# A graph layer and its feed-forward on one core: the neighbour sums of a block in two halves, in three bursts a slot, and a sixth of the rescalings on VectorE

## The chip, the cores and the metric

One core of a Trainium2 chip runs the kernel. The metric is device time in microseconds of one launch, over several runs. The profile is one profiled execution of the same program; its times are counted from its first instruction.

## What is computed

6250 nodes have 512 features each. 106,250 edges (50,000 random ones in both directions, and one from each node to itself) are sorted by their destination, so a node has 17 on average. Two layers follow each other:

```
xn  = layernorm(x)
agg = segment_sum(xn[src], dst);  neigh = agg / max(deg, 1)
h   = layernorm(xn @ W_self + b_self + neigh @ W_neigh) * gamma + beta
h   = where(h >= 0, h, 0.25 * h) + xn
x1  = x + h
y   = layernorm(x1)
out = x1 + (silu(y @ q(w_gate).T) * (y @ q(w_up).T)) @ q(w_down).T
```

`q` rounds each group of 128 weights to -1, 0 or 1 times the group's mean size. The feed-forward is 512 to 1408 to 512. Inputs and output are float32.

## The kernel before

**Blocks and slots.** The nodes are cut into 49 blocks of 128. A first stage (to about 205 us) normalises each block, multiplies it by `W_neigh` on TensorE in float32 (line 807) and writes the result to a table in HBM, split into a high and a low float16 part (2 x 512 values a node). The same stage turns the quantised weights around and finds, for each block, the first edge that ends in it (`edge_ranges`, VectorE, whose passes over 125 x 2450 values stand between blocks 9 and 16). Then come 49 slots `t`, one for each block, of 18 ticks `k`, and some more without a block. A slot is an order of work, not a time: each engine walks the same ticks and waits on semaphores.

**The sums of a block.** 2304 edges (18 tiles of 128, `STEPS`) cover a block. SyncE loads their sources (`idx`) and destinations (`dstv`) two slots ahead. GpSimd gathers one row of the table for each edge, by one indirect DMA for each tile (line 759), into `rows`, which holds 18 tiles: tile `j` of the next block may start when TensorE has used tile `j` of this one (`p_used`, in pairs). VectorE makes the one-hot matrix `hot` of the destinations (line 1293; 128 x 2304), and adds it up into `degs` in three reductions (line 1303). TensorE multiplies, for each tile, the one-hot matrix (as weights, 128 columns) with the high and with the low half of the gathered rows and adds both up in the bank `agg_ps` (lines 889 and 891): 36 products of 512 columns a block. `AGG_AT` spreads the 18 tiles over the ticks 2 to 17. At the next slot's tick 0 VectorE takes the sum out of the bank (line 1475, `v_h0`), which the first product of the next block waits for; then come the two norms of the block, and DMA transposes that put it into `x1T`.

**The feed-forward.** It runs on chunks of four blocks (512 columns; the first chunk has one block), interleaved with the sums. Each 128-row group of weights has its own scale, so a sum is built in a PSUM bank of `LANES` = 6 in turn: a step is two products (high and low part, lines 994 and 995) onto the bank, then the bank is multiplied by the ratio of two scales (line 1088 on ScalarE; line 1432 on VectorE, which does 2 of 5 only after the last block's slot), then the bank's next step may come. A list `FSTEPS` holds the steps, and `PACE` and `EVEN` (38 and 35 a slot) say to which tick each is assigned; a chunk can't begin before its last block is in `x1T`, and the list leaves a gap in the slot where nothing is ready. Products with `W_self` (line 807, float32) and the transposes of finished results (line 934) run among these steps. In slots 0 to 4 the place of the feed-forward is taken by 23 blocks of `W_self` products (`HELD_IN`).

## Time and profile before

| | us |
|---|---|
| median of 3 runs (lowest, highest) | 1694.86 (1693.52, 1698.13) |
| span of the profiled execution | 1674.1 |
| first stage | to about 205 |
| the block sums taken from the bank, first and last | 245.2 and 1552.6 |
| TensorE, VectorE, ScalarE, GpSimd busy | 1537.9, 1055.9, 1177.1, 938.3 |

The profiled span is 20.8 us under the median; that much lies around it. A product's duration (0.38 us) is its way through the array; products start closer together than that, so what TensorE can do is read from starts. A float32 product has two records. A GpSimd record is the writing of one gather's descriptors, and not the gather.

### The profile page before, as it was taken

How to read it: one execution, taken by the hardware profiler on the slowest of the kernel's cores; microseconds unless marked ns; L12 is line 12 of the kernel's file. 1: busy time of each engine (PE TensorE's matmuls, PEld its weight loads, DVE VectorE, ACT ScalarE, POOL GpSimd, SP SyncE). 2: the span in 40 equal slices, each digit the busy share in tenths (PEclk: the TensorE clock that was granted, in tenths of full speed). 3: DMA queues.
4: the chain of work that ended last, by engine and by line, in shares of the span. 5: the costliest groups of instructions: out<-in, count | busy, mean ns of one | idle time of the engine just before them, and what ended most of it. 6: DMA issues, size and time to landing. Idle time of an engine off the chain costs nothing.

```text
span 1674.1 us, 21796 instructions
## 1 busy us (share of the span) xinstructions
PE 1537.9 (92%) x6421; PEld 750.7 (45%) x6422; DVE 1055.9 (63%) x2305; ACT 1177.1 (70%) x2248; POOL 938.3 (56%) x936
## 2 busy tenths in 40 slices
PE   7999989987889999999999998999998998989897
PEld 3444434444444454444444444444444443444343
DVE  8999624655565565564665756557466466573876
ACT  5577500026777787778787786869887887879796
POOL 2123277666676666666666766667666666764000
PEclk9999989989998999999999999999999999999999
DMA  9869488997776887777777867787777777784101
GB/s 303 257 219 292 125 293 313 274 282 208 213 226 189 225 224 221 218 229 210 216 212 226 228 201 230 209 235 211 217 209 223 218 213 223 206 228 129 38 14 37
DMA packets 210883, 353.40 MB, mean 211 GB/s; under 512 B 105482, under 2 KB 105482, under 8 KB 210754
## 3 DMA queue, kind: packets, MB, share of 16 engines
q0 software_dynamic: 70560, 231.27, 47.4%
q1 hardware_dynamic: 140204, 120.73, 24.5%
q8 instruction: 52, 0.85, 0.2%
q14 instruction: 67, 0.55, 0.1%
HBM read 295.79 MB, written 39.62 MB: 200 GB/s over the span
## 4 chain that ended last, share of the span: by engine, by line
PE 84%; issue 6%; ACT 6%; DVE 2%; DMA 1%; another core or an unknown queue 0%; DVEq 0%; SPq 0%; ACTq 0%
PE f_ps L994 21%; PE f_ps L995 20%; PE f_ps L807 20%; PE agg_ps L889 10%; PE agg_ps L891 10%; ACT f_ps L1088 4%; PE side_ps L934 1%; PE agg_ps L803 1%; PE side_ps L803 1%; PE f_ps L889 0%; PE f_ps L891 0%; ACT hT L1113 0%; ACT acc L1098 0%; DVE acc L1440 0%; DMA rows<-in_x 0%
## 5 line engine op out<-in xcount | busy, mean ns | idle before, releaser
L759 POOL DMA_INDIRECT rows<-node_table,idx x882 | 891.6, 1011 | 442.6 <-issue 241.3
L1088 ACT ACTIVATE f_ps<-f_ps,ratio 128x512 f32<-128x512 f32 (+2 forms) x1303 | 777.0, 666 | 240.6 <-PE f_ps L995 163.2
L994 PE MATMUL f_ps<-x1T,tern 128*128 128x512 f16 (+2 forms) x1144 | 424.2, 374 | 52.0 <-issue 28.2
L995 PE MATMUL f_ps<-x1T,tern 128*128 128x512 f16 (+2 forms) x1144 | 422.4, 372 | 0.0
L889 PE MATMUL agg_ps<-rows,hot 128*128 128x512 f16 x846 | 328.5, 388 | 22.8 <-issue 22.8
L891 PE MATMUL agg_ps<-rows,hot 128*128 128x512 f16 x846 | 326.1, 385 | 4.3 <-issue 4.3
L1440 DVE SCALAR_TENSOR_TENSOR acc<-f_ps,scl,acc 128x512 f32<-128x512 f32 (+2 forms) x143 | 102.4, 717 | 229.0 <-PE f_ps L995 116.4
L994 PE MATMUL f_ps<-hT,tern 128*128 128x512 f16 (+2 forms) x572 | 213.4, 376 | 25.6 <-issue 13.0
L995 PE MATMUL f_ps<-hT,tern 128*128 128x512 f16 (+2 forms) x572 | 212.6, 374 | 0.0
L994 PEld LDWEIGHTS f_ps<-x1T,tern 128*128 128x128 f16 x1144 | 113.1, 99 | 216.6 <-issue 67.2
L889 PEld LDWEIGHTS agg_ps<-rows,hot 128*128 128x128 f16 x846 | 120.1, 142 | 133.3 <-issue 64.2
L995 PEld LDWEIGHTS f_ps<-x1T,tern 128*128 128x128 f16 x1144 | 113.9, 100 | 109.6 <-issue 7.1
L891 PEld LDWEIGHTS agg_ps<-rows,hot 128*128 128x128 f16 x846 | 121.6, 144 | 84.0 <-issue 39.9
L1453 DVE TENSOR_TENSOR hT<-acc,hT 128x512 f16<-128x512 f32 (+2 forms) x143 | 93.5, 654 | 84.9 <-issue 47.1
L1303 DVE TENSOR_REDUCE degs<-hot 128x44 f16<-128x792 f16 x147 | 133.1, 944 | 0.0
L1098 ACT ACTIVATE acc<-f_ps,scl 128x512 f32<-128x512 f32 (+2 forms) x143 | 98.4, 693 | 28.7 <-PE f_ps L995 23.1
L807 PE MATMUL f_ps<-wself,xj 128*128 128x512 f32 x208 | 107.3, 597 | 2.9 <-issue 1.7
L994 PEld LDWEIGHTS f_ps<-hT,tern 128*128 128x128 f16 x572 | 56.7, 99 | 116.1 <-ACT f_ps L1088 39.9
L737 POOL TENSOR_TENSOR hsx<-hsx 128x512 f16<-128x512 f16 x33 | 38.7, 1175 | 102.5 <-DVE hsx L1266 58.9
L1129 ACT ACTIVATE work<-x,nmn,rsn 128x512 f32<-128x512 f32 x49 | 41.6, 849 | 74.4 <-issue 54.0
L1113 ACT ACTIVATE hT<-acc 128x512 f16<-128x512 f32 (+2 forms) x143 | 90.3, 631 | 2.7 <-DVE acc L1440 2.4
L995 PEld LDWEIGHTS f_ps<-hT,tern 128*128 128x128 f16 x572 | 57.2, 100 | 55.4 <-issue 4.9
(176 smaller groups left out, 1705.1 us busy)
## 6 DMA issues: line engine op xcount, KB each, us to landing
rows<-node_table,idx POOLq DMA_INDIRECT x882
hsx<-own_rows SPq DMA_DIRECT2D x49, 256.0 KB
hsx<-in_x SPq DMA_DIRECT2D x48, 256.0 KB
out_nodes<-work SPq DMA_DIRECT2D x48, 256.0 KB, 2.2
xj<-xnt_rows SPq DMA_DIRECT2D x26, 256.0 KB
node_table<-work SPq DMA_DIRECT2D x25, 256.0 KB, 3.1
acc<-own_rows SPq DMA_DIRECT2D x23, 256.0 KB
own_rows<-acc SPq DMA_DIRECT2D x23, 256.0 KB
```

Source lines behind the costliest of these rows:

```text
L759: pool.indirect_dma_start(out=rows[:, j, :], out_offset=None, in_=table[:, :], in_offset=bass.IndirectOffsetOnAxis(ap=of[:, j:j + 1], axis ...
L807: return pe.matmul(to[:, :], turned_rows[:, k, :], weight[:, k, :], start=(k == 0), stop=(k == KT - 1), skip_group_check=True)
L889: pe.matmul(agg[:, :], hot[:, b % 2, :, j], rows[:, j, 0:D], start=(j == 0), stop=False, skip_group_check=True)
L891: mm = pe.matmul(agg[:, :], hot[:, b % 2, :, j], rows[:, j, D:2 * D], start=False, stop=(j == STEPS - 1), skip_group_check=True)
L994: pe.matmul(to, lhs, parts[0], start=g == 0, stop=False, skip_group_check=True)
L995: pe.matmul(to, lhs, parts[1], start=False, stop=True, skip_group_check=True).then_inc(p_ff, 1)
L1088: act.activation(ps, ps, ACT.Copy, scale=ratio[:, w if up else 2, j:j + 1]).then_inc(a_scaled, 1)
L1098: act.activation(acc[:, 0, u % 2, 0:width], ps, ACT.Silu, scale=scl[:, 0, j:j + 1]).then_inc(a_silu, 1)
L1113: act.activation(hT[:, 0, f, 0:width], acc[:, 1, u % 2, 0:width], ACT.Copy).then_inc(a_hi, 1)
L1303: dve.tensor_reduce(degs[:, lo:hi], hot[:, b % 2, lo:hi, :], AX.X, ALU.add).then_inc(v_degs, 1)
L1440: dve.scalar_tensor_tensor(out=acc[:, 1, u % 2, 0:width], in0=ps, scalar=scl[:, 1, j:j + 1], in1=acc[:, 0, u % 2, 0:width], op0=ALU.mult, ...
L1453: dve.tensor_tensor(hT[:, 1, f, 0:width], acc[:, 1, u % 2, 0:width], hT[:, 0, f, 0:width], ALU.subtract).then_inc(v_hlo, 1)
```

## The change

A block's 128 nodes become two halves of 64 (`HALVES`). A half gets a window of 11 tiles: half 1 the tiles 7 to 17, half 0 the tiles -1 to 9, of which -1 is left out. Tiles 7, 8 and 9 are in both. In each of 11 rounds TensorE multiplies one tile with the 64 one-hot columns of half 0, into the partitions 0 to 63 of `agg_ps`, and another with the 64 of half 1, into the partitions 64 to 127: 42 products with 64 columns of weights a block, where there were 36 with 128. A block whose halves don't fit their windows, or unsorted edges, go another way; with these inputs that happens in neither kernel.

The rounds run in three bursts, at the ticks 5, 12 and 17. `rows` has 22 tiles: a ring of 16 for the 15 that one half uses, and 3 twice for the shared ones. A tile comes free at the end of its burst (`freed_by`).

`hot` is now 11 x 128 (1408) a block, from `windows`, and `degs` comes from one reduction. The edges are loaded as rows (18 x 128), a slot earlier, turned around on TensorE (`turn_edges`, tick 2), and copied out by VectorE (`take_edges`, tick 3); both indices are float32 on the way. The degree product and ratio move to ticks 2 and 3, and results are turned out at ticks 5, 9 and 13 in place of 12 and 17. The first edges of the halves are found by two passes on GpSimd (850 and 4900 values a partition, block 9 of the first stage), 55 small products on TensorE at block 23, and short VectorE operations at block 25, in place of `edge_ranges`. `PACE` and `EVEN` are 42 and 39. VectorE takes each sixth rescaling during the block slots. A ring of banks in the first stage has 5 in place of 6, `x1` 11 tiles in place of 12. Slots 0 to 4 no longer use a second bank for the sums of odd blocks.

```diff
--- before.py
+++ after.py
...
-PER_LOAD = 2
-LOADS = STEPS // PER_LOAD
+HALVES, HN = 2, 64
+STRIDE, ROUNDS = 8, 11
+SINGLE_RING = 16
+RING = SINGLE_RING + 6
+DST_ROW = 32
+OSTEPS = 8
 TICKS = 18
-BIG = float(1 << 17)
+BIG = 1 << 14
+NO_NODE = -20000.0
 FAR = 20000.0
 
 
...
-    XJR, X1R = 2, 12
+    XJR, X1R = 2, 11
...
-    PACE, EVEN = 38.0, 35.0
+    PACE, EVEN = 42.0, 39.0
...
-    AGG_AT = [[] for _ in range(TICKS)]
-    for j in range(STEPS):
-        AGG_AT[2 + j * (TICKS - 2) // STEPS].append(j)
...
+    def tile_of(h, i):
+        return STRIDE * h - 1 + i
+
...
+    BURST_ROUNDS = [range(0, 4), range(4, 8), range(8, ROUNDS)]
+    BURST_AT = {5: 0, 12: 1, TICKS - 1: 2}
+    SHARED = [7, 8, 9]
+    ORDER = []
+    for i in range(ROUNDS):
+        ORDER += [j for j in (tile_of(1, i), tile_of(0, i)) if j >= 0 and j not in ORDER]
...
+    SINGLE = [j for j in ORDER if j not in SHARED]
...
+    FIRST_USE = {j: min(n for n, rounds in enumerate(BURST_ROUNDS) if any(tile_of(h, i) == j for h in range(HALVES) for i in rounds))
+                 for j in range(STEPS)}
+    ARRIVE = [sum(n == FIRST_USE[j] for j in ORDER) for n in range(len(BURST_ROUNDS))]
+
+    def row_at(b, j):
+        if j in SHARED:
+            return SINGLE_RING + len(SHARED) * (b % 2) + j - SHARED[0]
+        return (b * len(SINGLE) + SINGLE.index(j)) % SINGLE_RING
+
+    def freed_by(b, j):
+
+        if j in SHARED:
+            return used_all(b - 1)
+        before = b * len(SINGLE) + SINGLE.index(j) - SINGLE_RING
+        if before < 0:
+            return 0
+        return used_all(before // len(SINGLE)) + BURST_OF[SINGLE[before % len(SINGLE)]] + 1
+
+    def used_all(blocks):
+        return len(BURST_ROUNDS) * blocks
...
-            by = False if SLOT_OF[s] < BLOCKS else products % 5 in (1, 3)
+            by = products % 6 == 3 if SLOT_OF[s] < BLOCKS else products % 5 in (1, 3)
...
-    room = [(t, k) for t in range(BLOCKS + 8) for k in ((12, 17) if t < BLOCKS else (2, 11))]
+    room = [(t, k) for t in range(BLOCKS + 8) for k in ((5, 9, 13) if t < BLOCKS else (2, 11))]
...
-        rows = sb("rows", [P, STEPS, 2 * D], F16)
+        rows = sb("rows", [P, RING, 2 * D], F16)
...
-        hot = sb("hot", [P, 2, P, STEPS], F16)
-        node_j = sb("node_j", [P, P, STEPS], F16)
+        hot = sb("hot", [P, 2, ROUNDS, P], F16)
+        node_j = sb("node_j", [P, P], F16)
+        edges = sb("edges", [P, 2, P], F32)
...
+        def windows(b):
+
+            row = dstl[:, b % 4, 0:ROUNDS]
+            return bass.AP(row.tensor, row.offset, [list(row.ap[0]), [1, ROUNDS], [STRIDE, HALVES], [0, HN]])
+
+        def by_half(tile):
+            return tile.rearrange("p i (h n) -> p i h n", h=HALVES)
+
+        def edge_bank(b):
+
+            bank, at = (first_ps, b * P) if b < 2 else (side_ps, P)
+            return bank[:, at:at + P]
...
+                after(sp, p_edges, b - 1)
                 at = sp.value_load(rangei[0:1, b:b + 1], min_val=0, max_val=E)
-                sp.dma_start(idx[:, b % 2, :], src_pad[bass.ds(at, PASS)].rearrange("(p e) -> p e", p=P)).then_inc(
-                    ld_idx[b % 2], 16)
-                sp.dma_start(dstv[:, b % 2, :], dst_pad[bass.ds(at, PASS)].rearrange("(p e) -> p e", p=P)).then_inc(
-                    ld_dv[b % 2], 16)
+                sp.dma_start(edges[0:STEPS, b % 2, :], src_pad[bass.ds(at, PASS)].rearrange("(j p) -> j p", p=P)).then_inc(
+                    ld_edges[b % 2], 16)
+                sp.dma_start(edges[DST_ROW:DST_ROW + STEPS, b % 2, :], dst_pad[bass.ds(at, PASS)].rearrange("(j p) -> j p", p=P)).then_inc(
+                    ld_edges[b % 2], 16)
...
+                if i == RANGES_FROM + 14:
+                    pe.wait_ge(pool_counts, 1)
+                    for n in range(NSEG):
+                        pe.matmul(first_ps[:, 0:NQ], onesm[0:EP, :], hit[:, n, :], start=(n == 0), stop=(n == NSEG - 1))
+                    for n in range(5):
+                        mm = pe.matmul(first_ps[:, 2 * P:2 * P + EROW // 5], onesm[0:EP, :],
+                                       unordered[:, n * EROW // 5:(n + 1) * EROW // 5], start=(n == 0), stop=(n == 4))
+                    mm.then_inc(p_counts, 1)
+                if i == BLOCKS - 3:
+                    pe.wait_ge(v_rngi, 1)
+                    turn_edges(0)
+                    turn_edges(1)
...
-                pool.wait_ge(ld_idx[b % 2], 16 * (b // 2 + 1))
-                for load in range(LOADS):
-
-                    after(pool, p_used, (b - 1) * LOADS + load + 1 if b else 0)
-                    gather_load(idx[:, b % 2], load, gathered[load])
+                pool.wait_ge(v_idx, 2 * b + 2)
+                for j in ORDER:
+                    after(pool, p_used, freed_by(b, j))
+                    gather(row_at(b, j), idx[:, b % 4, j:j + 1], gathered[len(BURST_ROUNDS) * (b % 2) + FIRST_USE[j]])
...
-            def sum_step(b, j):
-                agg = sums(b)
-                if j == 0:
-                    pe.wait_ge(v_hot, b + 1)
-
-                    after(pe, v_h0, b - 1 if b < EARLY else b)
-                    if b == 1:
-                        pe.wait_ge(v_hsd, HELD_FIRST)
-                if j % PER_LOAD == 0:
-                    pe.wait_ge(gathered[j // PER_LOAD], (b + 1) * 16 * PER_LOAD)
-                pe.matmul(agg[:, :], hot[:, b % 2, :, j], rows[:, j, 0:D], start=(j == 0), stop=False,
-                          skip_group_check=True)
-                mm = pe.matmul(agg[:, :], hot[:, b % 2, :, j], rows[:, j, D:2 * D], start=False, stop=(j == STEPS - 1),
-                               skip_group_check=True)
-                if j % PER_LOAD == PER_LOAD - 1:
-                    mm.then_inc(p_used, 1)
+            def sum_burst(b, n):
+                pe.wait_ge(v_hot, b + 1)
+                if n == 0:
+                    after(pe, v_h0, b)
+                pe.wait_ge(gathered[len(BURST_ROUNDS) * (b % 2) + n], 16 * ARRIVE[n] * (b // 2 + 1))
+                for i in BURST_ROUNDS[n]:
+                    for part in range(2):
+                        for h in range(HALVES):
+                            if tile_of(h, i) < 0:
+                                continue
+                            lo = h * HN
+                            mm = pe.matmul(agg_ps[lo:lo + HN, :], hot[:, b % 2, i, lo:lo + HN],
+                                           rows[:, row_at(b, tile_of(h, i)), part * D:(part + 1) * D],
+                                           start=(part == 0 and i == (0 if h else 1)),
+                                           stop=(part == 1 and i == ROUNDS - 1), skip_group_check=True)
+                mm.then_inc(p_used, 1)
...
-                    if k == 6 and 0 < t < BLOCKS:
+                    if k == 2 and 0 < t < BLOCKS:
                         degree(t)
+                    if k == 2 and t + 2 < BLOCKS:
+                        turn_edges(t + 2)
                     if (t, k) in TURN_AT:
-                        turn_out(TURN_AT[t, k], min(t + 1, BLOCKS))
-                    if t < BLOCKS:
-                        for j in AGG_AT[k]:
-                            sum_step(t, j)
+                        turn_out(TURN_AT[t, k], t)
...
+                    if t < BLOCKS and k in BURST_AT:
+                        sum_burst(t, BURST_AT[k])
...
+            def take_edges(b):
+                dve.wait_ge(p_edges, max(b + 1, 2))
+
+                if b >= 4:
+                    dve.wait_ge(p_used, used_all(b - 3))
+                    dve.wait_ge(v_hot, b - 3)
+                bank_ = edge_bank(b)
+                dve.tensor_copy(idx[:, b % 4, :], bank_[:, 0:STEPS]).then_inc(v_idx, 1)
+                dve.tensor_scalar(dstl[:, b % 4, 1:STEPS + 1], bank_[:, DST_ROW:DST_ROW + STEPS], base_m[:, b:b + 1], None,
+                                  ALU.subtract).then_inc(v_idx, 1)
+
             def one_hot(b):
-                dve.wait_ge(ld_dv[b % 2], 16 * (b // 2 + 1))
-                after(dve, v_hot, b)
-                dve.tensor_scalar(dstl[:, :], dstv[:, b % 2, :], base_m[:, b:b + 1], None, ALU.subtract).then_inc(v_dl, 1)
-                dve.wait_ge(v_dl, b + 1)
-                after(dve, p_used, (b - 1) * LOADS)
-                dve.tensor_tensor(hot[:, b % 2, :, :], dstl[:, None, :].broadcast_to((P, P, STEPS)), node_j[:, :, :],
+                dve.wait_ge(v_idx, 2 * b + 2)
+                after(dve, p_used, used_all(b - 1))
+                after(dve, v_degs, b - 1)
+                dve.tensor_tensor(by_half(hot[:, b % 2]), windows(b), by_half(node_j[:, None, :].broadcast_to((P, ROUNDS, P))),
                                   ALU.is_equal).then_inc(v_hot, 1)
 
             def count_edges(b):
...
                 dve.wait_ge(v_hot, b + 1)
 
                 after(dve, p_deg, b)
-                for lo, hi in ((0, 44), (44, 88), (88, P)):
-                    with nc.allow_low_precision(reason="whole numbers up to STEPS"):
-                        dve.tensor_reduce(degs[:, lo:hi], hot[:, b % 2, lo:hi, :], AX.X, ALU.add).then_inc(v_degs, 1)
-                    yield
+                with nc.allow_low_precision(reason="whole numbers up to ROUNDS"):
+                    dve.tensor_reduce(degs[:, :], hot[:, b % 2].rearrange("p i m -> p m i"), AX.X, ALU.add).then_inc(v_degs, 1)```

In the orders below `f_ps` is a feed-forward bank, `tern` the turned weights, `x1T` and `hT` the two operands of its steps, `side_ps` a bank for degrees and turned results.

TensorE before, around the degree product of a slot in the middle:

```order
L877 MATMUL side_ps<-ones,degs 128x1
L889 MATMUL agg_ps<-rows,hot 128x512
L891 MATMUL agg_ps<-rows,hot 128x512
L994 MATMUL f_ps<-hT,tern 128x512
L995 MATMUL f_ps<-hT,tern 128x512
L994 MATMUL f_ps<-x1T,tern 128x512
L995 MATMUL f_ps<-x1T,tern 128x512
L889 MATMUL agg_ps<-rows,hot 128x512
L891 MATMUL agg_ps<-rows,hot 128x512
```

TensorE now, at the first burst of the same slot:

```order
L879 MATMUL f_ps<-wself,xj 128x512
L1088 MATMUL f_ps<-x1T,tern 128x512
L1089 MATMUL f_ps<-x1T,tern 128x512
L1088 MATMUL f_ps<-x1T,tern 128x512
L1089 MATMUL f_ps<-x1T,tern 128x512
L987 MATMUL agg_ps<-rows,hot 64x512 x14
L1088 MATMUL f_ps<-x1T,tern 128x512
```

The two products of each tile, one tile after each few steps, have become runs of 14, 16 and 12 half-wide products, with nothing but steps, a `W_self` product or a turn between.

VectorE before, from a block's second scaling to the last reduction of `hot`:

```order
L1523 SCALAR_TENSOR_TENSOR work<-work,rsn,beta_b 128x512
L1290 TENSOR_SCALAR dstl<-dstv,base_m 128x18
L1293 TENSOR_TENSOR hot<-dstl,node_j 128x2304
L1398 TENSOR_SCALAR inv<-side_ps,osc 128x1
L1400 RECIPROCAL inv<-inv 128x1
L1458 SCALAR_TENSOR_TENSOR hsx<-work,hsx 128x512
L1303 TENSOR_REDUCE degs<-hot 128x44 x2
L1303 TENSOR_REDUCE degs<-hot 128x40
```

VectorE now, at the same place:

```order
L1608 SCALAR_TENSOR_TENSOR work<-work,mvn,gamma_b 128x512
L1523 TENSOR_SCALAR f_ps<-f_ps,ratio 128x512
L1613 SCALAR_TENSOR_TENSOR work<-work,rsn,beta_b 128x512
L1382 TENSOR_TENSOR hot<-dstl,node_j 128x1408
L1549 SCALAR_TENSOR_TENSOR hsx<-work,hsx 128x512
L1391 TENSOR_REDUCE degs<-hot 128x128
```

The three reductions are one, `hot` is smaller, the degree ratio has gone to the slot's start, and rescalings of feed-forward banks (here line 1523) stand between the operations of the norm.

## Rows read from the trace of the kernel before

**Rows 1.** The page: busy time and share of each engine.
```profile
PE 1537.9 (92%) x6421; PEld 750.7 (45%) x6422; DVE 1055.9 (63%) x2305; ACT 1177.1 (70%) x2248; POOL 938.3 (56%) x936
```

**Rows 2.** The page: the chain that ended last, by engine.
```profile
PE 84%; issue 6%; ACT 6%; DVE 2%; DMA 1%; another core or an unknown queue 0%; DVEq 0%; SPq 0%; ACTq 0%
```

**Rows 3.** Stretches: busy us by engine (count), granted clock, DMA share, GB/s.
```profile
245.00:442.00 197.00, 171.91 (x732) 89.46 (x732) 104.59 (x251) 60.13 (x165) 133.97 (x134) 0.95 0.87 263
442.00:1552.00 1110.00, 1031.25 (x4502) 500.74 (x4501) 666.50 (x1463) 887.59 (x1507) 731.89 (x724) 0.98 0.75 214
1552.60:1674.00 121.40, 105.72 (x505) 49.04 (x503) 93.85 (x163) 95.65 (x162) 0.00 (x0) 0.96 0.09 31
```

**Rows 4.** Timeline of VectorE: the sum taken in slots 8 and 49 (start, us).
```profile
441.86 0.72 DVE L1475 SCALAR_TENSOR_TENSOR work<-agg_ps,inv,hsx 128x512 f32<-128x512 f32 x1
...
1552.64 0.74 DVE L1475 SCALAR_TENSOR_TENSOR work<-agg_ps,inv,hsx 128x512 f32<-128x512 f32 x1
```

**Rows 5.** Timeline of TensorE: products of sums and steps, start and duration.
```profile
897.98 0.38 PE L889 MATMUL agg_ps<-rows,hot 128*128 128x512 f16 x1
898.20 0.38 PE L891 MATMUL agg_ps<-rows,hot 128*128 128x512 f16 x1
898.42 0.38 PE L994 MATMUL f_ps<-x1T,tern 128*128 128x512 f16 x1
```

**Rows 6.** TensorE by line, 442 to 1552 us: count, busy, mean ns, idle before.
```profile
L994 PE MATMUL f_ps<-x1T,tern 128*128 128x512 f16 x901 | 347.1, 385 | 30.6 <-issue 15.8 <-ACT f_ps L1088 10.5 <-ACT yT L1103 0.8
L889 PE MATMUL agg_ps<-rows,hot 128*128 128x512 f16 x738 | 285.5, 387 | 19.7 <-issue 19.7
L994 PE MATMUL f_ps<-hT,tern 128*128 128x512 f16 x440 | 171.3, 389 | 22.2 <-issue 11.9 <-ACT f_ps L1088 9.6
L807 PE MATMUL f_ps<-wself,xj 128*128 128x512 f32 x144 | 73.7, 594 | 0.0
```

**Rows 7.** Timeline of TensorE in the first stage: four transposes, then float32 products.
```profile
63.48 0.60 PE L803 MATMUL agg_ps<-identf,x 128*128 128x128 f32 x4
63.92 3.60 PE L807 MATMUL f_ps<-acc,work 128*128 128x512 f32 x8
67.35 0.60 PE L803 MATMUL side_ps<-identf,x 128*128 128x128 f32 x4
```

**Rows 8.** Timeline of TensorE at a slot's end: it waits to refill the bank.
```profile
1473.12 0.38 PE L995 MATMUL f_ps<-x1T,tern 128*128 128x512 f16 x1
1475.23 0.41 PE L889 MATMUL agg_ps<-rows,hot 128*128 128x512 f16 x1 [1.73 <-issue]
```

**Rows 9.** Timeline of TensorE's weight loads (PEld), start and duration.
```profile
897.77 0.14 PEld L889 LDWEIGHTS agg_ps<-rows,hot 128*128 128x128 f16 x1
897.99 0.14 PEld L891 LDWEIGHTS agg_ps<-rows,hot 128*128 128x128 f16 x1
```

**Rows 10.** GpSimd: the gathers of 442 to 1552 us by line, then some in time.
```profile
L759 POOL DMA_INDIRECT rows<-node_table,idx x724 | 732.5, 1012 | 357.3 <-issue 186.4 <-PE agg_ps L891 94.2 <-remote 76.7
...
922.54 0.95 POOL L759 DMA_INDIRECT rows<-node_table,idx  x1 [0.31 <-issue]
923.80 0.94 POOL L759 DMA_INDIRECT rows<-node_table,idx  x1 [0.30 <-issue]
```

**Rows 11.** VectorE by line: the last row of 1552.6 to 1674 us, the others of 442 to 1552.
```profile
L1303 DVE TENSOR_REDUCE degs<-hot 128x44 f16<-128x792 f16 x80 | 75.1, 969 | 0.0
L1293 DVE TENSOR_TENSOR hot<-dstl,node_j 128x2304 f16<-128x2304 f16 x40 | 54.6, 1365 | 1.4
L1290 DVE TENSOR_SCALAR dstl<-dstv,base_m 128x18 f16<-128x18 f32 x40 | 10.1, 251 | 0.0
...
L1432 DVE TENSOR_SCALAR f_ps<-f_ps,ratio 128x512 f32<-128x512 f32 x33 | 24.5, 753 | 3.1 <-PE f_ps L995 2.6
```

**Rows 12.** ScalarE's rescalings, and GpSimd's elementwise operations (the page).
```profile
L1088 ACT ACTIVATE f_ps<-f_ps,ratio 128x512 f32<-128x512 f32 (+2 forms) x1303 | 777.0, 666 | 240.6 <-PE f_ps L995 163.2
L737 POOL TENSOR_TENSOR hsx<-hsx 128x512 f16<-128x512 f16 x33 | 38.7, 1175 | 102.5 <-DVE hsx L1266 58.9
```

323 lines of the change are left out of this document (177 added, 146 removed).

## The prediction

> **What bounds the kernel now.** I read the busy shares first, then the chain. TensorE is busy for 92% of the span, ScalarE 70%, VectorE 63%, GpSimd 56% [rows 1], and 84% of the chain that ended last is TensorE [rows 2]. A busy TensorE is not yet a full one, so I read starts. Products of the sums and of the steps both start 0.216 us apart (898.20, 898.42) though each lasts 0.38 [rows 5]: the price of a 512-column product is 0.216 us, and the weight loads of 0.14 us run under the product before (898.20 starts a product, 897.99 the load for it) [rows 9].
>
> The steady part is 442 to 1552 us, in which the sum is taken 41 times, first at 441.9, last before 1552.6 [rows 4]: 27.1 us a slot. What TensorE must do there, per slot: 1341 steps of two products (901 + 440 [rows 6]) are 32.7 a slot, x 0.431 = 14.1 us; 36 products of the sums x 0.2155 = 7.8; 144 float32 records at 0.43 (eight take the 3.43 us from 63.92 to 67.35 [rows 7]) are 1.5; transposes (four in 0.44 [rows 7]), one set a slot, 0.4. Together 23.8. The remaining 3.3 us are waits and clock. The granted clock is 0.98 [rows 3], so some 4% of the time was at 1.2 GHz in place of 2.4, which costs 2%, 0.5 us a slot. Next come steps that wait for a rescaling, and the bank of the sums: the first product of a block waits until VectorE has taken the last sum (1473.12 to 1475.23 [rows 8]; 19.7 us in all, 0.5 a slot [rows 6]).
>
> Beside it stands a second limit. GpSimd writes a gather in 1.012 us on the mean and needs 0.30 between two [rows 10]; 18 of them are 23.6 us a slot. It now waits for TensorE; but no slot can average under 23.6 us, whatever TensorE does.
>
> **The change, part by part.**
>
> *The sums.* 42 products with 64 weight columns in place of 36. If the two of a round run side by side, a block has 22 pair times (round 0 has one half only, two products; ten rounds have two pairs): 22 x 0.2155 = 4.7 us, 3.0 less a slot. The trace has no half-wide product, so a pair's price p is bounded from the rows: 0.2155 if side by side, 0.431 if one after the other, and more if a load no longer runs under a product (below). The rows nearest to it are the 128-wide products, whose different columns of the array already work at the same time in 0.2155; nothing in them shows two streams at once. I take 0.2155 and keep the others as rivals. The Trainium skill ("TensorEngine Tiling (Array Packing)", Key Properties) says that tiles of the array run loads and products in parallel, and "TensorE: Matmul & The Clock Gate", Part 3, gives 2.38 times the rate for three narrow tiles. No run here shows either yet; scaled to two tiles, that rate is an estimate of 0.27 for p, 1.2 us a slot more and some 1655 us.
>
> *The bursts.* Each slot enters and leaves the half-wide form three times. A product's way through the array beyond the next start is 0.38 - 0.216 = 0.165 us [rows 5]. If each of six changes lets the array run empty, that is 1.0 us; zero if none does; with a load of 0.14 laid bare as well [rows 9], 1.8. I take 1.0. The Trainium skill ("TensorEngine Tiling (Array Packing)", Key Properties) says too that changing the mode drains the array; by it 1.0 is right, without it the sum would be 41 us lower.
>
> *What moves on TensorE.* `turn_edges` is one small transpose, 0.11 us. The feed-forward has the same steps. The order puts 11 more of them ahead of the last block's slot (+0.1 us a slot, given back after it). Raising `PACE` from 38 to 42 does not bring work out of the end, since a chunk waits for its last block: the full slots get 42 and one of four gets a larger gap. TensorE per slot: 23.8 - 3.0 + 1.0 + 0.1 + 0.1 = 22.0 us.
>
> *What stays of the 3.3 us.* The wait at the bank should go, since the first burst is now at tick 5 and not at 2: -0.5. ScalarE loses a sixth of 26.2 rescalings a slot, 4.4 x 0.6 (777.0 / 1303 [rows 12]) = 2.6 us of its 21.6 (887.6 / 41 [rows 3]). VectorE has 16.3 (666.5 / 41 [rows 3]). Of that go the three reductions (2.8); in come one of 1408 values at 1.22 ns each (0.969 / 792), 1.7; `hot` falls from 1.37 to between 0.8 (same rate) and 1.7 (rate of the reductions), I take 1.2; two small copies for one, +0.25; 4.4 rescalings at 0.75, +3.3 [rows 11]. That makes 18.6, 74% of a 25 us slot. It has room, but it works in order: a rescaling behind `hot` and the reduction can be 3 us late, where six banks cover about six steps (2.6 us). I add 0.3. So 3.1 us remain, and a slot takes **25.1 us**, 2.0 less; 41 slots give -81 us.
>
> *Gathers.* GpSimd is then occupied 94% (23.6 of 25.1). A block's last eight tiles for the second burst can start only when the burst of the block before frees them (tick 12); they need 8 x 1.31 = 10.5 us and are due a slot later, 25 us after. This costs nothing as long as a slot is above 23.6. The edges are requested at tick 12 and needed at tick 2 of the next slot, about 11 us; the copies behind them are five small operations, whose cover is that time.
>
> *The early slots* (245 to 442 us, 197 us for seven [rows 3]). The same 2.0 us fall away in the long ones, but the short ones of this stretch are near 25 and can only go to 23.6: -13 us.
>
> *The first stage.* 50 products of 98 columns and 5 of 170: between 0.041 (a share of 0.2155) and 0.11 us each (a transpose [rows 7]), 2 to 6 us on the path, which is TensorE there (3.87 us a block [rows 7]). I take +3. The passes on GpSimd are 13,200 values a partition at 1.175 / 512 us [rows 12], 30 us, in the 54 us from block 9 to block 23. `edge_ranges` leaves VectorE, which runs behind there; that covers the loss of one bank.
>
> *The end* (121 us [rows 3]) has 11 steps less but a gap in slot 50: -2.
>
> Sum: 1674.1 - 81 - 13 + 3 - 2 = 1581; with 20.8 around the span, **1602 us**.
>
> **Rivals.**
>
> *A: the gathers become the bound.* If ScalarE's relief removes more of the waits, slots fall to the 23.6 us of GpSimd, say 23.9: 41 x -3.2 = -131, early -13, +1: 1552 us. For it: 94% occupancy already in the forecast. Against it: the waits of 3.3 us have stood beside a ScalarE at 80%, and it goes to 76% of a shorter slot. Chance 0.15.
>
> *B: the changes and VectorE take most of it.* Changes at 0.3 each (1.8 us) and late rescalings (+0.4): slot 26.3, -33, early -6: 1657 us. Chance 0.12.
>
> *C: slower, halves one after the other.* p = 0.431 for a pair, 42 products, 9.05 us: TensorE has 26.3, the slot 29.4, +2.3: +95 and +13 early: 1804 us. Its place is each burst, and it decides from p = 0.307, where 22p - 7.8 + 1.2 - 0.2 is zero: above it the kernel is slower. For it: no row shows two products in the array. Chance 0.07.
>
> *D: slower, loads laid bare.* In the half-wide form a load might have to wait until the product on its columns is through: p = 0.38 + 0.14 = 0.52, 11.4 us, slot 31.8: +193 and +30: 1918 us. Against it: now a load does run under a product on the same rows and columns [rows 9]. Chance 0.04. The Trainium skill ("TensorE: Matmul & The Clock Gate", Part 3) has a rule for this: loads overlap running products only if their row groups differ. All products here use all rows, and rows 9 contradict the rule for 128 columns; the half-wide form is open.
>
> That the change doesn't do what it says has no case of its own: the order shows the runs of 14, 16 and 12 half-wide products.
>
> **How the numbers follow.** The forecast has 0.62, A 0.15, B 0.12, C 0.07, D 0.04. The likeliest gives 1602 us; its own range is 1575 to 1635 (changes at 0 to 0.3 us, a first stage of 2 to 6, waits of 2.5 to 3.6). To hold 8 in 10 the range takes in A and B: 1550 to 1662. Within 0.3% (5 us, about what a measurement of this kernel can tell from no change) lies only a p near 0.307: 0.02. Slower: C and D, 0.11. Faster: 0.87.
>
> **What would show it.** In the changed kernel's timeline two half-wide products should start within some ns of each other and each pair 0.216 us after the last (C: 0.216 for each product; D: gaps between pairs with loads in them). Between the last half-wide product and the next step there should be some 0.38 us in place of 0.216. The sums taken should be 25.1 us apart on the mean, and GpSimd should still wait for TensorE, a little (A: for nothing). The wait of rows 8 should be gone. VectorE should be busy for about 18.6 us a slot, ScalarE 19.0. I am wrong if the pair price is off by more than 0.05 us (45 us over 41 slots), or if steps wait for VectorE by over a microsecond a slot.

## The result, and the profile after

The changed kernel takes **1896.27 us** (median of 3 runs, 1887.09 to 1898.24) against 1694.86: a ratio of 1.116, 95% interval 1.112 to 1.121. Forecast were 1602 us and a range of 1550 to 1662. The profiled execution has a span of 1896.5 us. By stage:

| | before, us | after, us | difference | forecast |
|---|---|---|---|---|
| start to the first sum taken | 245.2 | 257.3 | +12 | +3 |
| the next seven slots | 196.7 | 232.2 | +35 | -13 |
| 41 slots | 1110.7 | 1284.2 | +174 | -81 |
| the end | 121.5 | 122.8 | +1 | -2 |

A slot of the steady part takes 31.3 us in place of 27.1. The head of the page and the clock of 40 equal slices, after:

```profile
PE 1529.1 (81%) x6819; PEld 639.2 (34%) x6820; DVE 1176.7 (62%) x2453; ACT 1077.2 (57%) x2051; POOL 950.4 (50%) x944
...
PEclk9999999976997898888888989999888888998999
...
PE 60%; issue 12%; ACT 8%; DVE 8%; another core or an unknown queue 7%; DMA 3%; SPq 1%; DVEq 1%; ACTq 0%
```

Against [rows 1, 2] every engine is busy for a smaller share of its span: none became the bound. TensorE's part of the chain of work fell from 84% to 60%. The windows of the 41 slots (length, busy time of TensorE, its weight loads, VectorE, ScalarE and GpSimd with counts, granted clock, DMA share, GB/s), first of after, then of before:

```profile
489.50:1773.70 1284.20, 1017.30 (x4781) 401.37 (x4782) 786.21 (x1603) 794.54 (x1329) 724.12 (x723) 0.89 0.65 185
```

```profile
441.90:1552.60 1110.70, 1031.95 (x4504) 501.09 (x4503) 667.20 (x1464) 887.78 (x1508) 731.99 (x724) 0.98 0.75 214
```

The clock fell from 0.98 to 0.89 (a good fifth of the time at 1.2 GHz), and GpSimd is busy for 56% of the stretch in place of 66%.

**The half-wide products do what the forecast said.** The timeline of TensorE in one slot (start, us, line, form, count):

```profile
927.49 0.38 PE L1089 MATMUL f_ps<-x1T,tern 128*128 128x512 f16 x1
927.80 1.92 PE L987 MATMUL agg_ps<-rows,hot 128*64 128x512 f16 x16
929.65 0.39 PE L1088 MATMUL f_ps<-x1T,tern 128*128 128x512 f16 x1
```

Sixteen products are through after 1.92 us. Less the 0.38 of the last, eight pairs begin within 1.54 us, seven distances of 0.22: the price of a pair is the 0.2155 that the sum took. The two products of a pair start 3 or 4 ns apart (the view merges them; the trace has each). Into the form it is 0.31 us from start to start (927.49 to 927.80), 0.1 more than 0.216; back again also 0.1 more.

**The steps wait for products that are recorded as done.** Another slot, first TensorE, then what the other engines do at that time (in brackets the idle time ahead and what ended it):

```profile
899.88 0.39 PE L1088 MATMUL f_ps<-x1T,tern 128*128 128x512 f16 x1
...
900.10 0.38 PE L1089 MATMUL f_ps<-x1T,tern 128*128 128x512 f16 x1
...
902.26 0.38 PE L1089 MATMUL f_ps<-x1T,tern 128*128 128x512 f16 x1
...
903.63 0.39 PE L1088 MATMUL f_ps<-x1T,tern 128*128 128x512 f16 x1 [0.99 <-issue]
```

```profile
898.26 1.02 POOL L832 DMA_INDIRECT rows<-node_table,idx  x1 [0.30 <-issue]
...
899.58 0.95 POOL L832 DMA_INDIRECT rows<-node_table,idx  x1 [0.30 <-issue]
...
900.84 0.95 POOL L832 DMA_INDIRECT rows<-node_table,idx  x1 [0.30 <-issue]
...
901.49 0.75 DVE L1565 SCALAR_TENSOR_TENSOR work<-agg_ps,inv,hsx 128x512 f32<-128x512 f32 x1 [1.77 <-remote]
...
902.09 0.94 POOL L832 DMA_INDIRECT rows<-node_table,idx  x1 [0.30 <-issue]
...
902.91 1.24 ACT L1183 ACTIVATE f_ps<-f_ps,ratio 128x512 f32<-128x512 f32 x2 [3.56 <-PE f_ps L1089]
```

The last burst of a block ends, by its records, at 899.94. VectorE, idle, takes the sum at 901.49. The first step behind the burst ends at 900.48 (the product of 900.10), and ScalarE, idle for 3.56 us, rescales it only at 902.91. TensorE goes on until its six banks are used (902.26), and then waits itself. ScalarE and VectorE wait for TensorE's signal, TensorE waits for ScalarE, and GpSimd writes one gather after another all the while.

The trace also records when a semaphore is counted up, and that tells whose delay it is. Behind the product that ends at 900.48 the semaphore of the steps stands still until 902.89, and ScalarE starts 0.02 us after that; at nine in ten of the late rescalings counted below the engine starts within 25 ns of the semaphore's record. In the 41 slots 29% of the recorded signals of TensorE come more than 0.3 us after the last product that can have sent them, up to 10.0 us; before it is 33%, up to 4.6. The signals of ScalarE and VectorE come at most 16 ns after their instructions in both. So it is TensorE's signal that is late, and neither the engine that waits for it nor the signals of all engines.

To count this, each rescaling was laid beside its product (the 1716 steps of two products, 1378 of them with a rescaling, are all in both traces). I call one **late** if its engine had been idle for over 0.3 us and it begins over 0.5 us after the recorded end of its product. After: 128 late ones in 41 slots, 4.8 us each on the mean. **Before: 101, 3.2 us each.** They were there in the trace of before, and I had not seen them. One stands at [rows 8]. The step just ahead of the product of 1473.12 ends at 1473.07, and its rescaling (timeline of ScalarE, before) is at:

```profile
1477.86 0.66 ACT L1088 ACTIVATE f_ps<-f_ps,ratio 128x512 f32<-128x512 f32 x1 [2.12 <-PE f_ps L995]
```

Of all late rescalings (waited for and late) only 2 of after and none of before have GpSimd busy for less than 60% of the 2.5 us up to the product's end. A late stretch (late rescalings no more than 5 us apart) begins 6 or 7 gathers after GpSimd's last pause of over 0.45 us at the median, and in after never before the fifth.

### The profile page after: what moved, and what is told of

It is laid out like the page before. It is cut to its first block, busy times and chain, and to the rows that moved or that the text cites. A ratio compares the mean times of both kernels' runs of the same rounds, so it can differ in the third digit from the quotient of the medians.

```text
span 1896.5 us, 22767 instructions
## 1 busy us (share of the span) xinstructions
PE 1529.1 (81%) x6819; PEld 639.2 (34%) x6820; DVE 1176.7 (62%) x2453; ACT 1077.2 (57%) x2051; POOL 950.4 (50%) x944
## 4 chain that ended last, share of the span: by engine, by line
PE 60%; issue 12%; ACT 8%; DVE 8%; another core or an unknown queue 7%; DMA 3%; SPq 1%; DVEq 1%; ACTq 0%
PE f_ps L1088 16%; PE f_ps L1089 16%; PE f_ps L879 16%; PE agg_ps L987 10%; ACT f_ps L1183 5%; DMA x1T<-hsx 2%; DVE f_ps L1523 1%; PE side_ps L1030 1%; DVE acc L1531 1%; DVE degs L1391 1%; ACT hT L1208 1%; ACT acc L1193 1%; DVE hot L1382 1%; PE agg_ps L875 1%
## 5 line engine op out<-in xcount | busy, mean ns | idle before, releaser
L832 POOL DMA_INDIRECT rows<-node_table,idx x882 | 881.9, 1000 | 663.4 <-PE agg_ps L987 329.4
L1183 ACT ACTIVATE f_ps<-f_ps,ratio 128x512 f32<-128x512 f32 (+2 forms) x1106 | 662.6, 645 | 469.7 <-PE f_ps L1089 269.9
L1088 PE MATMUL f_ps<-x1T,tern 128*128 128x512 f16 (+2 forms) x1144 | 444.4, 393 | 204.3 <-issue 72.6
L1089 PE MATMUL f_ps<-x1T,tern 128*128 128x512 f16 (+2 forms) x1144 | 443.7, 392 | 0.0
L1523 DVE TENSOR_SCALAR f_ps<-f_ps,ratio 128x512 f32<-128x512 f32 (+2 forms) x272 | 196.5, 723 | 266.8 <-PE f_ps L1089 172.1
L1088 PE MATMUL f_ps<-hT,tern 128*128 128x512 f16 (+2 forms) x572 | 229.1, 403 | 78.3 <-ACT f_ps L1183 39.7
L987 PE MATMUL agg_ps<-rows,hot 128*64 128x512 f16 x2058 | 276.0, 401 | 1.6 <-issue 1.6
L1088 PEld LDWEIGHTS f_ps<-x1T,tern 128*128 128x128 f16 x1144 | 116.2, 102 | 434.8 <-issue 208.2
L1089 PE MATMUL f_ps<-hT,tern 128*128 128x512 f16 (+2 forms) x572 | 227.3, 400 | 0.0
L987 PEld LDWEIGHTS agg_ps<-rows,hot 128*64 128x64 f16 x2058 | 115.9, 114 | 158.1 <-issue 82.1
L1089 PEld LDWEIGHTS f_ps<-x1T,tern 128*128 128x128 f16 x1144 | 117.8, 103 | 106.1 <-issue 28.5
L879 PE MATMUL f_ps<-wself,xj 128*128 128x512 f32 x208 | 123.5, 679 | 8.7 <-ACT yT L1198 3.2
L1088 PEld LDWEIGHTS f_ps<-hT,tern 128*128 128x128 f16 x572 | 59.9, 105 | 201.0 <-issue 71.7
L1391 DVE TENSOR_REDUCE degs<-hot 128x128 f16<-128x1408 f16 x49 | 125.1, 2553 | 0.0
L1565 DVE SCALAR_TENSOR_TENSOR work<-agg_ps,inv,hsx 128x512 f32<-128x512 f32 x49 | 36.7, 749 | 87.3 <-remote 74.5
L1089 PEld LDWEIGHTS f_ps<-hT,tern 128*128 128x128 f16 x572 | 60.0, 105 | 61.6 <-issue 21.2
```

Of the source, the lines that this page charges most:

```text
L832: pool.indirect_dma_start(out=rows[:, at, :], out_offset=None, in_=table[:, :], in_offset=bass.IndirectOffsetOnAxis(ap=of, axis=0)).then_i ...
L879: return pe.matmul(to[:, :], turned_rows[:, k, :], weight[:, k, :], start=(k == 0), stop=(k == KT - 1), skip_group_check=True)
L987: mm = pe.matmul(agg_ps[lo:lo + HN, :], hot[:, b % 2, i, lo:lo + HN], rows[:, row_at(b, tile_of(h, i)), part * D:(part + 1) * D], start=(p ...
L1088: pe.matmul(to, lhs, parts[0], start=g == 0, stop=False, skip_group_check=True)
L1089: pe.matmul(to, lhs, parts[1], start=False, stop=True, skip_group_check=True).then_inc(p_ff, 1)
L1183: act.activation(ps, ps, ACT.Copy, scale=ratio[:, w if up else 2, j:j + 1]).then_inc(a_scaled, 1)
```

## The experiments

The theories: **G**, GpSimd's gathers make TensorE's completions arrive late. Against it **V**, VectorE is late because it works in order; **P**, the pace of 42 leaves TensorE idle in one slot of four; **M**, the changes of form. All slots below are means of the last 41, between takings of the sum; times of before beside them, in the same jobs, were 1693 to 1698 us. Where a run has no ratio, its time is that of a single execution. A run without the gathers, with half their bytes or rows, or with plain loads leaves out or replaces rows that the sums need, from block 8 on.

### Which part costs it

Without gathers, from block 8 on:

```diff
                 for j in ORDER:
                     after(pool, p_used, freed_by(b, j))
-                    gather(row_at(b, j), idx[:, b % 4, j:j + 1], gathered[...])
+                    if b >= 8:
+                        pool.sem_inc(no_gather[FIRST_USE[j]], 1)
+                    else:
+                        gather(row_at(b, j), idx[:, b % 4, j:j + 1], gathered[...])
...
```

> The changed kernel without the gathers of blocks 8 to 48: GpSimd only counts a semaphore up at the same places, and the sums of these blocks use old rows (the output is therefore not the reference's). Theory G (TensorE's completions are signalled late, up to some 10 us, whenever GpSimd's gathers run): rescalings no longer start over 0.5 us after the recorded end of their product in slots 9 to 48, no clock below 0.95 in most slots, slot 25 us or less, about 1896 - 41 x 6 = 1650 us. Theory V (VectorE is late because it works in order): slots stay above 30 us, over 1850 us. Theory P (the pace of 42 a slot): over 1850 us.

Measured: 1594.3 us, slot 24.2, not one late rescaling, clock 0.98; no signal of TensorE is over 0.05 us late. G holds (its time was forecast 56 us too high), and V and P fall: the order, the pace, the bursts and VectorE's load are all still there.

```diff
-            by = products % 6 == 3 if SLOT_OF[s] < BLOCKS else products % 5 in (1, 3)
+            by = False if SLOT_OF[s] < BLOCKS else products % 5 in (1, 3)
```

> The changed kernel with all rescalings of the block slots on ScalarE again. Theory V: the waits of 5 us for a VectorE rescaling behind the reduction (2.55) and hot (1.62) go, slot 28 us, about 1760 us. Theory G: VectorE only shows what comes late from TensorE; the time stays within 25 us of 1896 or gets longer by ScalarE's 2.6 us a slot (up to 2000).

Measured: 1904 to 1932 us, ratio to before 1.130 (1.119 to 1.140), slot 32.2. V had forecast 1760, and is wrong. That VectorE's rescalings were a small help is likely and no more: the interval just meets that of the changed kernel (1.112 to 1.121).

```diff
-    PACE, EVEN = 42.0, 39.0
+    PACE, EVEN = 38.0, 35.0
```

> The changed kernel with PACE and EVEN at 38 and 35 as before. Theory P (the packed slots leave a gap of 6 to 10 ticks in one slot of four, where TensorE falls to half clock): the three long slots and the short one come together, clock from 0.89 to over 0.95, about 1780 us. Theory G: within 30 us of 1896.

Measured: 1882 us, 1.111 (1.104 to 1.118), slot 31.7, clock 0.90, 166 late. P is wrong.

```diff
-    BURST_ROUNDS = [range(0, 4), range(4, 8), range(8, ROUNDS)]
-    BURST_AT = {5: 0, 12: 1, TICKS - 1: 2}
+    BURST_ROUNDS = [range(n, min(n + 2, ROUNDS)) for n in range(0, ROUNDS, 2)]
+    BURST_AT = {5: 0, 8: 1, 10: 2, 12: 3, 15: 4, TICKS - 1: 5}
...
-        BURST_OF[j] = 2
+        BURST_OF[j] = len(BURST_ROUNDS) - 1
```

> The changed kernel with the eleven rounds in six bursts (ticks 5, 8, 10, 12, 15, 17) in place of three. Theory G with lumps (a burst frees eight rows at once, so eight gathers in a row meet the steps behind it): gathers are spread, signals late as often as in the kernel before, slot 27 to 28 us, 1700 to 1760 us. Theory M (each change between half-wide and full products costs the time): twice the changes, slot 33 us, about 1960 us. Theory V: no change, within 25 us of 1896.

Measured: 1855 us, 1.097 (1.089 to 1.104), slot 30.7, 159 late. Twice the changes of form, and it is faster, so M is wrong. But the time that G forecast for it is missed by 95 us too: with six bursts 26% of the stretches of ten gathers still come at under 1.5 us a gather, against 30% with three.

### What in the gathers

The same cut in the kernel before (no gathers from block 8 on):

> The kernel before without the gathers of blocks 8 to 48 (old rows in their place, the output is not the reference's). Theory G (completions of TensorE are signalled late while gathers run, in both kernels): the 101 late rescalings fall to nearly 0 and the slot from 27.1 to 25 or 26 us, 1610 to 1650 us; the changed kernel without gathers took 1594, so the half-wide sums are then still the faster ones. If only bursts bring the lateness: within 10 us of 1695.

Measured: 1556.8 us, slot 24.15, none late: more than G had forecast. The windows of the 41 slots of this kernel, and of the changed one without gathers:

```profile
443.20:1433.30 990.10, 982.84 (x4506) 515.61 (x4504) 660.42 (x1466) 887.41 (x1508) 0.00 (x0) 1.00 0.17 48
```

```profile
478.00:1470.30 992.30, 917.03 (x4791) 394.49 (x4790) 782.03 (x1604) 787.14 (x1329) 0.00 (x0) 0.98 0.17 47
```

Before, without gathers, is TensorE alone: busy 99%, full clock, 24.15 us against the 23.8 summed up in the prediction. So 2.9 of the 3.3 us of "waits and clock" of a slot came with the gathers. The slot is the same in both kernels: the half-wide sums take 66 us of busy time off TensorE (982.8 to 917.0, 1.6 a slot), and gain nothing. G's last claim, that they are still the faster ones, was wrong.

Half the bytes:

```diff
-                    out=rows[:, at, :], out_offset=None, in_=table[:, :],
+                    out=rows[:, at, 0:D if half else 2 * D], out_offset=None,
+                    in_=table.rearrange("n (h d) -> (n h) d", h=2) if half else table[:, :],
...
```

> The changed kernel, each gather of blocks 8 to 48 with 512 of the 1024 values of a row (same number of gathers and of rows, half the bytes; the low halves of the rows are old, the output is not the reference's). Theory G1 (what makes TensorE's signals late is the bytes that the gathers move): less than half of the 128 late rescalings, slot 25 to 27 us, 1620 to 1700 us. Theory G2 (it is GpSimd's writing of descriptors or their number): late as before, slot 30 us or more, over 1840 us.

Measured: 1883.5 us, slot 31.3, 146 late. Not the bytes.

Plain loads in place of the gathers:

```diff
...
+                        pool.dma_start(rows[:, row_at(b, j), :], table[b * P:(b + 1) * P, :]).then_inc(s, 16)
...
```

> The changed kernel with a plain load of 128 adjacent rows of the table in place of each gather of blocks 8 to 48 (same bytes, same semaphores, no index; the sums are of other rows, the output is not the reference's). Theory G1 (bytes, or the writes into the memory that TensorE reads): late as before, slot 29 us or more, over 1800 us. Theory G2 (the gather's own descriptors): hardly a late rescaling, slot 24 to 25 us, 1590 to 1640 us.

Measured: 1654.5 us, slot 25.7, none late, at 225 GB/s in the slots (185 with gathers). The same bytes into the same memory, and no signal is late. The slot is 1.5 us longer than without gathers, a time just above G2's range; TensorE waits for `x1T` for 84.9 us there (29.7 without gathers), which is most of it. GpSimd writes such a load in half the time of a gather (line, count, busy, mean ns, idle and what ended it; of this kernel's page):

```profile
L865 POOL DMA_DIRECT2D rows<-node_table x738 | 390.4, 537 | 661.9 <-PE agg_ps L991 648.3
L832 POOL DMA_INDIRECT rows<-node_table,idx x144 | 143.0, 993 | 108.9 <-issue 53.2
```

Gathers of 64 rows in place of 128:

```diff
-                    out=rows[:, at, :], out_offset=None, in_=table[:, :],
-                    in_offset=bass.IndirectOffsetOnAxis(ap=of, axis=0)).then_inc(s, 16)
+                    out=rows[0:count, at, :], out_offset=None, in_=table[:, :],
+                    in_offset=bass.IndirectOffsetOnAxis(ap=of[0:count], axis=0)).then_inc(s, 16)
...
```

> The changed kernel, each gather of blocks 8 to 48 with 64 in place of 128 rows (same number of gathers, half the rows and bytes; the other 64 partitions keep old rows, the output is not the reference's). Half the bytes alone changed nothing. Theory D (each row of a gather, that is each descriptor GpSimd writes, is what delays TensorE's signals): under 30 late rescalings (128 before), slot 25 to 27 us, 1620 to 1700 us. Theory I (it goes by the gather instruction, whatever it holds): over 100 late, over 1830 us.

Measured: 1864.5 us, slot 30.6, 122 late. The one execution is 32 us under the changed kernel's median, but the lateness stays: it goes by the gather, not by its rows.

### The bursts alone, the sixth alone

```diff
     for j in range(STEPS):
-        AGG_AT[2 + j * (TICKS - 2) // STEPS].append(j)
+        AGG_AT[(5, 12, TICKS - 1)[j // 6]].append(j)
```

> The kernel before with its sums in three bursts of six tiles (twelve 128-wide products) at the ticks 5, 12 and 17, nothing else changed. Theory L (lumps: rows come free in lumps, the gathers follow in lumps and meet the steps that come after the burst): slot 30 to 31 us, 1820 to 1870 us. Theory H (it is the half-wide form, with two products and two weight loads in 0.216 us): slot 27 to 28 us, 1690 to 1740 us.

Measured: 1787.9 us, ratio 1.058 (1.052 to 1.064), slot 29.4, clock 0.95. With 128-wide products: the bunching alone costs 2.3 of the 4.2 us a slot. It lies between both forecasts (L 1820 to 1870, H 1690 to 1740), so L has the mechanism and not the size; the rest belongs to what else the change brings. GpSimd's waits, by line and what it waited for (total us, times, longest), after and before:

```profile
POOL rows L832 <- PE agg_ps L987: 329.4, 71, 11.1
```

```profile
POOL rows L759 <- PE agg_ps L891: 104.4, 87, 3.1
```

GpSimd stands still up to 11 us until a burst frees rows, and then has to write its gathers without a break.

```diff
-            by = False if SLOT_OF[s] < BLOCKS else products % 5 in (1, 3)
+            by = products % 6 == 3 if SLOT_OF[s] < BLOCKS else products % 5 in (1, 3)
```

> The kernel before with each sixth rescaling of the block slots on VectorE, nothing else changed. Theory G (the steps wait for TensorE's late signals, not for ScalarE, which only looks busy because it catches up): within 10 us of 1695. Theory S (ScalarE at 80% is what the steps wait for between the late stretches): slot 26 to 26.5 us, 1650 to 1680 us. Theory V (VectorE's rescalings come late): 1710 to 1760 us.

Measured: 1699.4 us, ratio 1.003 (1.001 to 1.006), 146 late. G is right: in the kernel before, relief for ScalarE brings nothing.

### How fast is too fast

A pause after every fourth gather (the short one has 2 fills, the long one 4), in the changed kernel; in the one before it stands at the same places:

```diff
+                    in_a_row += 1
+                    if in_a_row % 4 == 0:
+                        for _ in range(4):
+                            pool.memset(zeros[:, :], 0.0).then_inc(pool_c, 1)
+                            idles += 1
+                            pool.wait_ge(pool_c, 5 + idles)
```

> The changed kernel with a pause of GpSimd after every fourth gather: two small fills one after the other, about 0.5 us. In both traces no series of late completions begins before the fifth gather in a row. Theory R (it is the unbroken row of gathers that makes TensorE's signals late, and a short pause clears it): under 20 late rescalings (128 before), slot 25 to 26 us, 1630 to 1700 us. If 0.5 us is too short a pause to clear it: over 100 late rescalings, 1870 to 1910 us. Theory C (late signals need the gathers but not a row of them): over 100 late rescalings, over 1850 us.

> The changed kernel with a pause of about 1.1 us (four fills) after every fourth gather. GpSimd then needs 18 x 1.25 + 4.5 x 1.1 = 27.5 us a slot and becomes the bound. Theory R: under 10 late rescalings, slot 27 to 28 us, 1720 to 1770 us. Theory C: slot 31 to 34 us, over 1890 us.

> The kernel before with the same pause of about 0.5 us after every fourth gather (18 x 1.25 + 4.5 x 0.5 = 24.8 us a slot on GpSimd). Theory R: the 101 late rescalings fall under 20, slot 25 to 26 us, 1610 to 1650 us: faster than both kernels. Theory C: 1690 to 1720 us.

> The kernel before with a pause of about 1.1 us after every fourth gather; GpSimd becomes the bound with some 27.5 us a slot. Theory R: hardly a late rescaling, slot 27.5 to 28 us, 1700 to 1730 us. Theory C: late rescalings as before and a later gather on top, over 1730 us.

Measured: 1796.7, 1792.4, 1705.8 and 1774.0 us. The changed kernel gains 100 us from being held up (ratios to before 1.060 and 1.057 in place of 1.116); the one before gains nothing (1.006 and 1.046). The short pause clears nothing (164 and 120 late), the long one nearly all (16 and 1). GpSimd is then the bound at 29.3 to 29.7 us a slot (52% and 53% of the chain that ended last): the long pause makes 2.45 us of one distance of 1.25 in four, and with all else four gathers take 6.5 to 6.6 us. Theory R, that an unbroken row is what does it, fails on the short pause, which breaks the row and clears nothing; theory C, that gathers are enough, fails on the long one. Of their times only C's for the short pause in the kernel before came true (1690 to 1720). Why the changed kernel gains 2 us a slot from the short pause, with 164 rescalings late (by 3.3 us each in place of 4.8), is not shown.

So fills after every gather, with no long pause anywhere (the last two runs with a second fill after each third or sixth gather):

```diff
                         in_offset=bass.IndirectOffsetOnAxis(ap=of[:, j:j + 1], axis=0)).then_inc(s, 16)
+                    if s is not o_rows:
+                        pool.memset(zeros[:, :], 0.0).then_inc(pool_c, 1)
+                        fills[0] += 1
+                        pool.wait_ge(pool_c, 5 + fills[0])
```

> The kernel before with one fill (0.34 us) after every gather: 1.59 us from gather to gather, and never a pause of a microsecond. Theory A (average rate: TensorE's signals fall behind when gathers come faster than one in 1.5 to 1.6 us, as with 1.25 and 1.42, and not at 1.62, the run with the long pauses): under 20 late rescalings, slot 28.6 to 29 us by GpSimd, 1735 to 1765 us. Theory W (only a pause of about 1.5 us clears it): over 60 late rescalings, over 1760 us.

> The kernel before with one fill after every gather and two after every third: 1.61 us from gather to gather on the mean, no pause over 1.1 us. The lateness began after about 6 gathers in a row at 1.25 us each and after about 31 at 1.45, which a backlog explains that grows by the gather's own time of about 1.50 us less the interval. Theory A (average interval against 1.50): under 10 late rescalings, slot 29.0 us by GpSimd, 1740 to 1765 us. Theory W (only a pause of about 1.5 us clears it): over 60 late rescalings, over 1765 us.

> The kernel before with one fill after every gather and two after every sixth: 1.53 us from gather to gather on the mean. Theory A with 1.50 us: under 30 late rescalings (120 at 1.45, 101 in the kernel before), slot 27.6 to 27.9 us, 1700 to 1715 us. Theory W, or a gather's own time of 1.55 or more: over 60 late rescalings, slot 28 us or more, 1715 to 1740 us.

Measured: 1705.9 us with 120 late; 1782.4 with 0; 1759.1 with 1. One fill is cheaper than planned (0.20 us; the timeline of GpSimd in the first of these):

```profile
901.63 0.95 POOL L761 DMA_INDIRECT rows<-node_table,idx  x1 [0.27 <-POOL zeros L765]
902.58 0.22 POOL L765 MEMSET zeros<- 128x128 f16 x1
903.07 0.95 POOL L761 DMA_INDIRECT rows<-node_table,idx  x1 [0.27 <-POOL zeros L765]
```

1.44 us from gather to gather, and the signals are late. In the other two the intervals came out longer than planned (1.65 for 1.61 in the one of 1782 us, 1.62 for 1.53 in the one of 1759), and GpSimd is the bound (54% of the chain of the one with 1759 us, where TensorE has 13%). Both times are above theory A's, but its count is right: with a second fill now and then, and hardly a pause of 1.5 us, the lateness is gone, so theory W falls.

Put together, with each gather's interval taken over ten in a row (the mean interval is the slot by 18 gathers, and tells no more than the slot):

| kernel | mean interval, us | tens of gathers under 1.5 us each | late rescalings | slot, us |
|---|---|---|---|---|
| before | 1.51 | 54% | 101 | 27.1 |
| before, short pauses | 1.55 | 33% | 120 | 27.8 |
| before, a fill each | 1.54 | 38% | 120 | 27.8 |
| before, bursts | 1.62 | 36% | 94 | 29.4 |
| before, long pauses | 1.63 | 6% | 1 | 29.25 |
| before, fills (1759 us) | 1.62 | 3% | 1 | 29.2 |
| before, fills (1782 us) | 1.65 | 0% | 0 | 29.6 |
| changed | 1.74 | 30% | 128 | 31.3 |
| changed, short pauses | 1.64 | 30% | 164 | 29.3 |
| changed, long pauses | 1.65 | 7% | 16 | 29.7 |

**Lateness goes with the local rate of the gathers**, not with the mean over a slot and not with a pause of a certain length. Kernels with 30% or more of their tens under 1.5 us have 94 to 164 late ones, those with 7% or less have 0 to 16. Within the first group the share tells nothing of the number. The onset fits a backlog: it begins after 6 gathers at 1.25 us, and at 1.44 after 28 at the median (about 31 in the expectation). If the backlog grows by c less the interval with each gather, 6 x (c - 1.25) = 28 x (c - 1.44) gives c = 1.49 us. That is an estimate; the backlog itself is in no record, and it doesn't give the size: a slot's 18 gathers at 1.25 us would add up to some 4 us, and rescalings come up to 11.2 us late. Eighteen gathers at 1.49 us are 26.8 us: by this estimate **a slot of before, 27.1 us, sits at the bound already.**

### Where the half-wide sums' gain went

The changed kernel without gathers, and with all rescalings on ScalarE:

> The changed kernel without the gathers of blocks 8 to 48 (output not the reference's) and with all rescalings of the block slots on ScalarE. Without the gathers both kernels had the same slot, 24.2 us, though TensorE has 1.6 us less to do a slot in the changed one. Theory V (that gain goes into steps that wait for VectorE, late behind the reduction and hot): slot 22.5 to 23.5 us, 1530 to 1565 us. Theory S (ScalarE's relief is needed): slot 24.5 to 25.5 us, 1605 to 1650 us. Neither, if it goes into chunk starts and results turned out: 1585 to 1600 us.

Measured: 1579.2 us, slot 24.0 (24.2 with the sixth). Moving VectorE's rescalings away is worth 0.2 us a slot, not 1.7: V falls here too, and so does S. The time is just under the 1585 to 1600 forecast for neither. The waits of TensorE in the changed kernel without gathers (steps at L1095, results turned out at L1037):

```profile
PE f_ps L1095 <- DMA x1T<-hsx: 29.7, 9, 5.4
PE side_ps L1037 <- issue: 22.0, 16, 2.3
PE f_ps L1095 <- DVE f_ps L1530: 11.1, 14, 2.0
PE f_ps L1095 <- ACT f_ps L1190: 7.3, 16, 0.6
```

The kernel before, without gathers, has some 7 us of such waits in all. Nine of the chunks now begin by waiting for the transposed block (29.7 us, up to 5.4 each): with less work to do TensorE is there early, and a chunk can't begin before its last block has gone through. I have tried nothing that separates this wait from the one at the turned-out results.

No version here that computes the whole result beats the kernel before.

## Why the prediction was wrong, point by point

- **The pair's price** (0.2155) and **the changes of form**: right, the latter 0.1 us each and not 0.165. TensorE's work without gathers is 917.0 / 41 = 22.4 us a slot, forecast 22.0. By the Trainium skill ("TensorEngine Tiling (Array Packing)", Key Properties) tiles of the array load and multiply in parallel and a change of mode drains the array; the trace agrees with the first (two products in 0.216 us), and 0.1 us is what a drain can have cost here.
- **The load rule** of the Trainium skill ("TensorE: Matmul & The Clock Gate", Part 3), by which loads overlap only with products of other row groups: the trace disagrees for this form too. Every half-wide product uses all rows, and pairs follow at 0.216 us with two loads each (the trace has a pair's loads 0.21 us ahead of it, under the pair before).
- **Rivals C and D** were wrong in mechanism, and D's 1918 us nearly right by accident. The total says nothing of the cause; the starts 0.22 us apart refute both.
- **"What stays of the 3.3 us"**: the step that failed first. I put the wait of [rows 8] down to the bank of the sums and let it go with the later first burst. It was a late signal of TensorE: VectorE came late to take the sum (1474.39) because a step ahead of it, through at 1471.78, was signalled so late that VectorE, idle for 3.19 us, began on it at 1473.72. Without gathers the whole 3.3 us fall to 0.35. They were one thing, and it grew from 2.9 to about 7 us a slot (31.3 less 24.2).
- **Gathers** ("costs nothing as long as a slot is above 23.6"): the step that turned the sign. In the kernel before the bursts alone cost 2.3 us a slot, where I had a gain of 2.0; without gathers the changed kernel's 31.3 fall to 24.2. I took GpSimd's record of 1.012 + 0.30 us as the gather's whole price. What it costs the others begins below some 1.5 us from gather to gather. The kernel before had its rows freed in pairs and wrote one in 1.51 us on the mean; the bursts made GpSimd wait up to 11 us and then write at 1.25. I saw that these gathers would have 25 us for 10.5 us of work, and took this for slack, while it has no effect on when they are written.
- **Rival A** was right in kind, with the price off: not 23.6 but, by the estimate above, about 27 us a slot. If that holds, no relief of TensorE could have gained anything; the kernel before with a sixth of the rescalings on VectorE, which gained nothing, agrees, but it relieved ScalarE and not TensorE.
- **VectorE**: 786.2 / 41 = 19.2 us a slot against 18.6. The reduction takes 2.55 us (1.7 forecast, 1.81 ns a value) and `hot` 1.62 (1.2). It mattered little: the feared microsecond a slot of steps that wait for VectorE was 11.8 us behind its rescalings in the 41 slots (0.3 a slot).
- **ScalarE**: 794.5 / 41 = 19.4 (19.0). Its idle time grew for lack of signals.
- **The clock**: I had it at 0.98. It fell to 0.89, and without gathers was 0.98: so the waits brought it down, and part of TensorE's work then ran at 1.2 GHz on top of them.
- **First stage and early slots**: +12 and +35 us against +3 and -13. The early slots have the same gathers; what the cheaper ring of banks and the lost second bank cost there was not tried.
- **Around the span** I added 20.8 us. The changed kernel's profiled execution took 1898.24 us for a span of 1896.5, 1.7 around it. So the profiled execution of before was likely a faster one than its median. That term touches both kernels alike and not the difference.

What the runs leave open: by what path a gather of GpSimd holds up TensorE's signals, and whether the 1.9 us a slot beyond the bunching come from the half-wide form, from the degree and edges moved to ticks 2 and 3, or from the longer idle stretches at half clock. Also, each run here carries its profile records; none tells whether the recording has a part in it. The recording is itself thinner beside the gathers: in the 41 slots the trace of before has 758 semaphore records of ScalarE, and 1398 without gathers, for the same work. And a plain load differs from a gather in more than the index: GpSimd writes it in 0.54 us in place of 0.99.
